# Two small attention layers: projections as three products of split operands, and the queries' rotary sum on GpSimd

## The reference, cut to what matters

```python
x = x + xattn0(layernorm(x), ctx, ctx)     # "xattn0": queries from x, keys and values from 32 rows of the context
x = x + attn0(layernorm(x))                # "attn0": all three from x
# each:
q = (xn @ Wq + bq); k = (kv @ Wk + bk); v = (kv @ Wv + bv)      # 256 x 256 weights, 16 heads of 16
q, k = rope(q), rope(k)                                          # x*cos + swapped(x)*sin
p = softmax(q @ k.T / 4, causal)                                 # 32 x 32 per head and batch row
x = x + (p @ v) @ Wo + bo
```

## Time and profile before

| | |
|---|---|
| Times of three runs | 1001.86, 1005.84, 1007.35 us; median 1005.84 |
| The profiled execution | 1011.99 us, span of its instructions 1010.2 us |
| Busy: PE / DVE / ACT / POOL | 915.6 / 642.6 / 434.0 / 361.8 us |
| Mean granted TensorE clock | 0.956 of 2.4 GHz |
| The two small layers | about the first 276 us of the span |

### The profile page before, as it was taken

One profiled execution on the slowest core, in us unless ns is written; L12 is line 12 of the kernel. 1 busy time (PEld: TensorE's weight loads), 2 busy tenths in 40 slices (PEclk: granted clock), 3 DMA queues, 4 the chain that ended last, 5 costly groups with the idle time before them and its releaser, 6 DMA issues.

```text
span 1010.2 us, 38856 instructions
## 1 busy us (share of the span) xinstructions
PE 915.6 (91%) x15864; PEld 744.6 (74%) x15894; DVE 642.6 (64%) x1718; ACT 434.0 (43%) x1150; POOL 361.8 (36%) x602
## 2 busy tenths in 40 slices
PE   4899899989847889999999999999878889999998
PEld 3777677877633678888888888888646568999976
DVE  5788688887795376667666766676577282233226
ACT  1322223322364555556555655565553313333331
POOL 6232213322198063333342232224056214555530
PEclk9999899999767999999999999999988799999999
DMA  7002400000001011111111111110056001222216
GB/s 252 24 24 60 142 4 3 5 4 4 3 0 48 2 49 50 50 50 50 55 69 70 51 49 50 50 49 3 2 193 261 22 17 61 72 70 73 75 57 241
DMA packets 29901, 60.92 MB, mean 60 GB/s; under 512 B 6000, under 2 KB 22480, under 8 KB 26416
## 3 DMA queue, kind: packets, MB, share of 16 engines
q1 hardware_dynamic: 25136, 48.00, 13.6%
q0 software_dynamic: 3744, 10.23, 3.0%
q10 hardware_dynamic: 864, 0.36, 0.2%
HBM read 49.27 MB, written 9.31 MB: 58 GB/s over the span
## 4 chain that ended last, share of the span: by engine, by line
PE 74%; issue 9%; DVE 8%; ACT 4%; POOL 3%; DVEq 1%; DMA 0%; ACTq 0%; another core or an unknown queue 0%; POOLq 0%
PE psum L827 13%; PE psum L1589 7%; PE psum L1600 7%; PE psum L903 7%; PE psum L261 5%; PE psum L234 4%; PE psum L300 3%; PE psum L890 3%; PE psum L1468 3%; PE psum L276 3%; PE psum L291 3%; PE psum L918 3%; ACT x_p L987 2%; PE psum L742 2%; PE psum L869 1%
## 5 line engine op out<-in xcount | busy, mean ns | idle before, releaser
L987 ACT ACTIVATE x_p<-x_s,x_nmax 128x257 f32<-128x257 f32 x256 | 127.5, 500 | 98.9 <-DVE x_nmax L1020 98.9
L1051 DVE COPY x_pT<-psum 128x512 f32<-128x512 f32 x128 | 88.2, 689 | 55.8 <-PE psum L903 53.9
L1020 DVE CUSTOM_DVE_ANT_0 x_s<-psum,x_mask 128x257 f32<-128x257 f32 x256 | 94.3, 423 | 41.2 <-PE psum L890 40.5
L1076 POOL TENSOR_TENSOR x_ctx1l<-x_ctx,x_ctx1h 128x2064 fp32r<-128x2064 f32 x8 | 36.8, 4601 | 144.1 <-ACT x_ctx1h L770 144.1
L903 PE MATMUL psum<-ident,x_p 128*128 128x128 f32 x512 | 80.0, 279 | 5.6 <-ACT x_p L987 1.8
L1650 DVE TENSOR_TENSOR me_out<-psum,me_eb 128x256 f32<-128x256 f32 x39 | 16.6, 425 | 91.0 <-PE psum L1600 91.0
L1600 PE MATMUL psum<-me_w,me_out 128*128 x312 | 73.6, 379 | 0.0
L903 PEld LDWEIGHTS psum<-ident,x_p 128*128 128x128 f32 x512 | 57.9, 141 | 17.1 <-ACT x_p L987 15.6
L918 PEld LDWEIGHTS psum<-x_v,x_pT 128*32 128x32 f32 x4096 | 47.7, 112 | 29.5 <-DVE x_pT L1051 18.5
L1076 POOL TENSOR_TENSOR x_ctx0l<-x_ctx,x_ctx0h 128x2064 fp32r<-128x2064 f32 x7 | 32.2, 4603 | 103.0 <-ACT x_ctx0h L770 103.0
L1005 DVE TENSOR_SCALAR x_k<-psum,x_bk 128x258 f32<-128x258 f32 x128 | 57.6, 481 | 13.1 <-PE psum L827 13.1
(11 more groups left out here) (284 smaller groups left out, 2535.1 us busy)
## 6 DMA issues: line engine op xcount, KB each, us to landing
x_ctx<-in_ctx SPq DMA_DIRECT2D x16, 1032.0 KB, 4.9
me_w<-in_moe_w SPq DMA_DIRECT2D x8, 1024.0 KB, 12.2
me_got<-moe_outs SPq DMA_DIRECT2D x8, 512.0 KB, 8.2
x_mask<-in_mask SPq DMA_DIRECT2D x16, 128.5 KB, 4.6
x<-in_x SPq DMA_DIRECT2D x4, 512.0 KB, 8.3
sm_cT<-in_ctx SPq DMA_DIRECT2D x16, 128.0 KB, 2.5
moe_rows<-me_xn SPq DMA_DIRECT2D x4, 512.0 KB, 6.0
me_ws<-in_moe_ws SPq DMA_DIRECT2D x1, 1024.0 KB, 4.8
```

Source lines behind the costliest of these rows:

```text
L987: nc.scalar.activation(x1_p[:, n, :], x1_s[:, rg, :], ACT.Exp, bias=x1_nmax[:, par, n:n + 1], scale=-1.0, accum_out=x1_sum[:, par, n:n + 1 ...
L1020: nc.vector.tensor_tensor_reduce(out=x1_s[:, rg, :], in0=psum[:, 2 + rg, 0:SK], in1=x1_mask[par][:, b, :], scale=1.0, scalar=-2 * MASKED, ...
L1051: nc.vector.tensor_copy(x1_pT[:, c].rearrange("p r k s -> p (r k s)"), psum[:, 6, :]).then_inc(x1["pT_ready"], 1)
L1076: eng.tensor_tensor(low[:], x1_ctx[:], high[:].bitcast(F32), ALU.subtract).then_inc(x1["ctx_split"], 1)
```

## The change

What it does, by engine:

- TensorE: each float32 product of the four projections becomes three float32r products (`exact`, `parts`). In attn0 the query and key products are one matmul of 512 columns.
- The operands are split. Transposed x and transposed head outputs: ScalarE's copy out of PSUM now writes the high part, and a new VectorE instruction subtracts it from PSUM for the low part (`xT_split`, `oT_split`). Context: ScalarE writes the high part (`context_high`), GpSimd the low part (`context_low`), one 128 x 256 instruction each a tile of xattn0. Weights: once a layer, xattn0 on ScalarE (`w_high`) and VectorE (`w_low`), attn0 on GpSimd at tiles 4, 6 and 9.
- The rotary sum of the queries goes from VectorE to GpSimd.
- The `pool_rstd` groups 1 to 3 of the first layer move from ahead of GpSimd's loop to its tiles 0, 1 and 2.
- Buffers of the transposed operands, queries and keys go from four to two, with their waits; the SBUF places of the weights move. DMAs are the same.

```diff
+        def w_high(eng, c, n):
+            w, high, _ = w_part(c, n)
+            eng.wait_ge(c.weights_loaded if n else c.qkv_loaded, 16 * 3 if n else 16)
...
+        def w_low(eng, c, n):
+            w, high, low = w_part(c, n)
+            eng.wait_ge(c.w_high, n + 1)
+            if n:
+                eng.wait_ge(c.bias_product, 1)
+            eng.tensor_tensor(low[:], w[:], high[:].bitcast(F32), ALU.subtract).then_inc(c.w_split, 1)
+
+        def context_low(pool, t):
+            pool.wait_ge(sm["cT_high"], t + 1)
+            nc.gpsimd.tensor_tensor(sm_cTs[1][:, t % 2], sm_cT[:, t % U], sm_cTs[0][:, t % 2].bitcast(F32),
+                                    ALU.subtract).then_inc(sm["cT_split"], 1)
```

TensorE:

```diff
                     if t > 0:
-                        pe.wait_ge(sm["xT_ready"], t)
+                        pe.wait_ge(sm["xT_split"], t)
...
-                    pe.wait_ge(sm["xT_ready"], t + 1)
+                    pe.wait_ge(c.w_split, 1)
+                    pe.wait_ge(sm["xT_split"], t + 1)
...
+                    else:
+                        for k in range(KC):
+                            exact(psum[:, QK + t % 2, :], parts(own(sm_xTs, k), [w[:, k, 0:2 * D] for w in c.w_qkvs]), k == 0, False,
+                                  skip_group_check=True)
```

ScalarE, ahead of its loop and at the end of a step:

```diff
+            w_high(nc.scalar, smalls[0], 0)
+            context_high(0)
...
                 if live(2):
                     t, u = n(2)
                     act.wait_ge(sm["shifted"], t + 1)
                     nc.scalar.activation(sm_p[:, u, :], sm_p[:, u, :], ACT.Exp, scale=DH ** -0.5).then_inc(sm["exp_ready"], 1)
+                if live(0):
+                    t, u = n(0)
+                    if t == 0:
+                        w_high(nc.scalar, smalls[0], 1)
+                    if 0 < t < NT - 1:
+                        context_high(t + 1)
```

VectorE, behind `sm_o` and ahead of the residual sum; then behind the row maximum; then the sum that went:

```diff
+                if live(0):
+                    t, u = n(0)
+                    dve.wait_ge(sm["xT_ready"], t + 1)
+                    nc.vector.tensor_tensor(sm_xTs[1][:, t % 2].rearrange("p k s -> p (k s)"), psum[:, XT, 0:D],
+                                            sm_xTs[0][:, t % 2].rearrange("p k s -> p (k s)").bitcast(F32),
+                                            ALU.subtract).then_inc(sm["xT_split"], 1)
...
+                if live(4):
+                    t, u = n(4)
+                    dve.wait_ge(sm["oT_ready"], t + 1)
+                    nc.vector.tensor_tensor(sm_oTs[1][:, t % 2].rearrange("p k s -> p (k s)"), psum[:, OUT, 0:D],
...
                 if live(1):
                     t, u = n(1)
-                    dve.wait_ge(sm["rope_parts"], 3 * (t + 1))
-                    nc.vector.tensor_tensor(sm_q[:, t % 2, :], sm_cosd[:, t % 2, 0, :], sm_sind[:, t % 2, 0, :],
-                                            ALU.add).then_inc(sm["q_roped"], 1)
```

GpSimd:

```diff
+            context_low(pool, 0)
             for t in range(len(smalls) * NT):
                 r, c = t % NT, layer(t)
+                if t + 1 < NT:
+                    context_low(pool, t + 1)
+                pool.wait_ge(sm["rope_parts"], 3 * (t + 1))
+                if t > 1:
+                    pool.wait_ge(sm["qT_ready"], t - 1)
+                nc.gpsimd.tensor_tensor(sm_q[:, t % 2, :], sm_cosd[:, t % 2, 0, :], sm_sind[:, t % 2, 0, :],
+                                        ALU.add).then_inc(sm["q_roped"], 1)
+                if 0 <= t < NT // U - 1:
+                    pool_rstd(pool, x_stats, U * (t + 2), t + 1)
+                if t == 4:
+                    w_high(nc.gpsimd, smalls[1], 0)
```

VectorE's start, behind the statistics of the first four tiles and ahead of those of the other twelve:

```diff
                     small_bias(nc.vector, smalls[0])
+                    w_low(nc.vector, smalls[0], 0)
```

More of the change, by code:

```diff
@@ L251, in step @@
                     c = layer(t)
-                    kv = sm_cT if c.cross else sm_xT
-                    pe.wait_ge(c.qkv_loaded, 16)
-                    pe.wait_ge(sm["xT_ready"], t + 1)
+                    own = lambda vs, k: [v[:, t % 2, k, :] for v in vs]
+                    pe.wait_ge(c.w_split, 1)
+                    pe.wait_ge(sm["xT_split"], t + 1)
                     if t > 1:
@@ L1720, in build @@
             f8_total = scratch("f8_total", [P, 2, U])
+            scratch("f8_room", [P, 4])
+            for c in smalls:
+                c.w_qkv = scratch(f"{c.name}_w_qkv", [P, KC, 3 * D])
+                c.w_o = scratch(f"{c.name}_w_o", [P, KC, D])
             f8_int = scratch("f8_int", [P, KC * D], I32)
```

102 lines of the change are left out of this document (65 added, 37 removed).

## The result

The changed kernel takes 1020.09 us (median of 4 runs, 1017.67 to 1020.76); the kernel before took 1006.6 us (median of 4, 1001.86 to 1012.34). The ratio is 1.0119, with a 95% interval of 1.0079 to 1.0159: 1.2% slower. The forecast was 1001 us, 0.5% faster, with a range of 989 to 1017. The sign was wrong, and the result lies above the range.

What follows compares the result with a forecast made beforehand. TensorE was taken to bound the kernel, VectorE 8% behind. Terms: attn0 -4.6, xattn0 -1.0, start +3.0, FP8 weights +1.0, stalls -3, together -4.6 us; off 1005.84 that gives 1001 us. Overall range 989 to 1017, the forecast's own 996 to 1006.

Steps and rivals of the forecast that it cites:

- TensorE's new step: Small layers: float32r products shorten TensorE's own step from 6.89 us to 6.29 in xattn0 and 6.19 in attn0.
- VectorE becomes the bound: Steady step: VectorE's floor rises from 6.08 to 6.37 us, above TensorE's new step; at most 0.52 us can be had.
- The new wait, 6.45, and the step of 6.6 us in attn0: Loop through ScalarE's copy, VectorE's first subtraction and TensorE takes 6.45 us a step; with some tenths of waits, 6.6.
- GpSimd: Queries' sum beside keys' sum: VectorE first, nothing lost in attn0; in xattn0 the context's subtraction costs VectorE about 0.3 us.
- The start, +3.0: Tile 0's first product waits for its low part on VectorE: 18.0 us instead of 14.97, +3.0 us.
- Of the 26.7 us of stalls TensorE can now catch up a little: Tiles 4 to 31: TensorE's idle 0.4 us a step wins back an estimated ninth of its stalls, -3 us.
- Draining steps, "the same": 0: Tiles 28 to 31 draining: one hop more and shorter products, as in the filling steps; nothing taken for the two.
- xattn0, 6.8 us a step, -1.0: First layer: step 6.8 us (bounds 6.4 and 7.4); 11 steps from tile 4 at 0.09 us saved, -1.0 us.
- attn0, -4.6: Second layer: 16 steps, each 0.29 us shorter, -4.6 us in all.
- Nothing moved in the layers behind but their start.: Sign to look for: layers behind the small ones change only in when they start.
- More slow clock: Rival, chance 0.10: TensorE idles more, four more slow-clock places at some 1.7 us each, 1008 us.
- GpSimd first: Rival, chance 0.20: queries' sum goes before keys' sum, VectorE loses 0.57 us a step, 1016 us.

Runs made afterwards that it cites:

- qsum_back: The changed kernel with the queries' rotary sum back on VectorE instead of GpSimd: ratio 1.0253 to the kernel before.
- out_f32: The changed kernel with the output projection alone as a float32 product again, without VectorE's subtraction for it: ratio 1.0005 to the kernel before.
- two pairs of profiles: First pair: one profile each of the kernel before and the changed kernel. Second: both once more, unedited, ratios 0.9997 and 1.0121 to the kernel before.
- more_tensor: The changed kernel with four needless float32 products of 128 columns in each of 14 first-layer steps: ratio 1.0084 to the kernel before.
- tail_f32: The changed kernel with the output projection of the last five tiles (27 to 31) in float32: ratio 1.0052 to the kernel before.
- attn_only: The kernel before with only the second layer's query, key and value products split, and the queries' sum on GpSimd in both layers: ratio 0.9906.
- qsum_only: The kernel before with the queries' rotary sum moved to GpSimd, the `pool_rstd` groups moved too, and no product split: ratio 0.9986.

## Why the prediction was wrong

By its own steps:

- **TensorE's new step.** Right: 0.12 us for 256 columns and 0.23 for 512, where 0.12 and 0.22 stood. The chain's pieces of a quiet attn0 step add up to 6.35 us, forecast 6.19.
- **VectorE becomes the bound.** Half right. It is nearly as full as TensorE, and 0.39 us given back to it (qsum_back) cost 13 us. But neither engine alone is the bound: the chain goes through both in turn.
- **The new wait, 6.45, and the step of 6.6 us in attn0.** Right for quiet steps: 13.24 us for two, others 6.47 to 6.96. But the loop was drawn for the subtraction of x^T alone; that of o^T went in as 0.34 us of VectorE and not as a hop, and the output projections' split cost 12 us (out_f32).
- **GpSimd.** Right in attn0, as the row at 74.93 had it: VectorE first, 0.42 us. Right in xattn0 too: "about 0.3 us on VectorE" came as 0.76 us for the keys' sum instead of 0.43.
- **The start, +3.0.** Nearly right: first product at 17.75 for 18.0. Nothing was taken for the filling steps: tile 0's rotary product is 2.2 and 2.3 us late in the two pairs of profiles, tile 4's 2.8 and 4.9, and tile 6's 5.4 and 7.8. So filling costs 3 to 5 us behind the start.
- **"Of the 26.7 us of stalls TensorE can now catch up a little": -3. This is the step that failed, and with it the nothing taken for filling and draining.** It took the number and length of the waits, and the half clock behind them, as given by the kernel before, and let them shrink. They grew. TensorE's idle time ahead of the attention products went from 12.4 to 20.7 us in the first pair of profiles and from 11.0 to 23.2 in the second. The time at 1.2 GHz ahead of the FP8 layer, 17 to 27 us in four profiles of the kernel before, was 34 and three times 51 in four of the changed one; over the whole span it is 28 us more, on average of the executions of one session. Half of 28 is 14 us, about what lies between the steps' sum without this term (-1.6) and the 12 us that the runs show (1.0121 of 1011.7). This fits in size and isn't a proof: half clock costs its half only where TensorE sets the pace, and more_tensor says that it doesn't in the first layer. Nor does each pair show it alike. In the first pair tiles 4 to 31 took 7.2 us less than before, which is what the terms promised (-4.6 - 1.0 + 1.0 - 3 = -7.6), and the waits for nothing and the half clock of tiles 0 to 31 hadn't grown; in the second pair they took 1.6 us more.
- **Draining steps, "the same": 0.** Wrong by 5 us (27 to 32, with 20 us at 1.2 GHz instead of 10; so a part of this half clock is in the 14 us above too), mostly put back by tail_f32. The hop for o^T was counted in the steady step and not in the drain; by the runs above it is some 2 to 4 us of the 5, and waits for nothing are the others.
- **xattn0, 6.8 us a step, -1.0.** Wrong: the quiet steps took 6.7 to 7.2 us in the first profile, most of them more than before's 6.89, and the layer as a whole lost 10 us by its split.
- **attn0, -4.6.** The split of the query, key and value products alone is worth 8 us (attn_only against qsum_only), more than forecast; with the output projection split too, 2.3 us are left of it (116.7 and 118.3 against 119.0 and 120.6).
- **"Nothing moved in the layers behind but their start."** From the first FP8 row to the end the same code took 726.9 and 729.2 us before, 734.7 and 731.2 after, with a clock of 0.96 and 0.95 against 0.94 and 0.95. In the first pair of profiles 7.7 of the 8.8 us lie there, in the second pair 2.0 of 13.2. Of the profiles of all kernels here this stretch took between 726.7 and 734.7. It moves by chance, and on average of four profiles each (padded ones too) it is 3 us longer in the changed kernel; whether that comes with the split stays open.
- **The rivals.** "More slow clock" is nearest to what the runs show; I gave it a chance of 0.10 and four places at 1.7 us. What I held against it, that idle of tenths never shows a low clock, was beside the point: in tiles 0 to 31 nearly all low stretches begin at single waits of over 1 us, most of them for nothing, and in the changed kernel's drain a long one begins at a wait of 0.93 us for VectorE's subtraction of o^T. "GpSimd first" named 1016 us, near the result, and for a reason that the row at 201.71 refutes in attn0.

What is shown is which parts cost how much, and that the changed kernel has more waiting and more half clock. What stays open is how the 12 us divide between the waits for other engines, the waits for nothing and the half clock, and why the waits for nothing are longer in most profiles (16.4 to 19.7 us over tiles 0 to 31 in four of the changed kernel, 11.9 to 17.5 in four of before). Their places are settled (multiples of 256 instructions). Whether it is the time between the bursts that the load of the next block needs was not measured by itself.

## What to carry to other kernels

Splitting products pays part by part or not at all: here it paid 8 us for attn0's query, key and value products, and cost 12 us for the output projections and 10 for the first layer, though each split saves TensorE time. So measure each part by itself, and count the hop that the split operand makes over a second engine where the pipeline fills and drains. Before you promise a gain on a TensorE that is nearly always busy, list its waits for nothing and its half clock, and treat them as a term that can grow when its work shrinks. A few needless matmuls show in one run whether TensorE's work sets the pace at all. Take two profiles of each kernel before you lay a difference of some us to a stage: here the same program's first 16 tiles took 112 and 119 us.

## What the runs showed of the hardware

- TensorE's waits for nothing over 1 us come at multiples of 256 instructions of its stream (126 matmul records and as many weight loads), last up to 2.9 us in a burst of short matmuls, and move by half a period with 128 added instructions.
- An increment of a semaphore by TensorE isn't free: 128 of them moved the first rotary product by 15.8 us in the kernel before, 256 by 35.7. The second 128 took 19.9 us (20.0 in the changed kernel), 0.16 us each.
- 12 us of added TensorE work (14 steps of 0.9 us) cost one kernel 11 us and the other nothing.
- A hop over VectorE in the draining pipeline cost some 2 to 4 us for its few tiles, and the clock was lower with it (0.68 in the drain against 0.81 in tail_f32 and before).
- Where GpSimd's subtraction was under way (0.72 us at 92.71), VectorE's sum of two SBUF operands took 0.76 us instead of 0.43; where both sums started together (201.7), VectorE kept its 0.42 and GpSimd took 0.98.
